# A four-layer graph kernel on one core: the input projected ahead of the first pass, and the second pass's first pieces loaded slot by slot

## The reference, cut to what matters

```python
# layer 0
h = jnp.maximum(_layernorm(x), 0.0)
A = a * adj + (1 - a) * I;  inv = 1 / A.sum(axis=1)
x = x + relu((inv[:, None] * A @ h) @ W0.T + b0)
# layer 1
h = jnp.maximum(_layernorm(x), 0.0)
XW = mobius_matvec(W1, h)                  # rows of h @ W1, rescaled by their norms
x = x + expmap0(relu(logmap0(mean(adj @ (gamma * XW), adj @ (gamma - 1)))))
# layer 2
h = jnp.maximum(_layernorm(x), 0.0) @ W2.T + b2
x = x + max over the rows h[topk_idx],  topk_idx = top_k(adj, 32)
# layer 3: as layer 1, with adj + I and a normalisation by degrees, then @ W3 + b3
```

## Time and profile before

| | us |
|---|---|
| three runs, median | 4701.98 |
| lowest, highest | 4695.71, 4706.68 |
| the profiled execution's own time | 4705.08 |
| its span, first to last instruction | 4703.3 |
| TensorE busy | 3573.1 (76% of the span) |
| VectorE, ScalarE, GpSimd busy | 2523.1, 1609.0, 2261.2 |

### The profile page before, as it was taken

How to read it: one execution, slowest core, us unless ns; L and a number is a source line. 1 busy time by engine, 2 the same in 40 slices (tenths; PEclk the granted TensorE clock), 3 DMA queues, 4 the chain that set the end, 5 groups by cost and what they waited for, 6 DMA issues and landing times.

```text
span 4703.3 us, 75636 instructions
## 1 busy us (share of the span) xinstructions
PE 3573.1 (76%) x29444; PEld 3486.2 (74%) x29444; DVE 2523.1 (54%) x5491; ACT 1609.0 (34%) x3554; POOL 2261.2 (48%) x2023
## 2 busy tenths in 40 slices
PE   6999999999999998576685771266666555666695
PEld 6999999999999998576685771266665555565695
DVE  5678878878878210343423416354444335344567
ACT  5777878778786221111201102111100000000114
POOL 4898989899897002334324324533333433323200
PEclk9999999999999999787886885587777777777897
DMA  7999999999999887465574662255555554555673
GB/s 240 332 393 363 385 359 381 356 386 379 367 389 360 283 292 261 154 230 179 199 248 154 221 219 82 84 201 180 178 188 168 171 179 156 176 188 181 207 252 106
DMA packets 401321, 1155.19 MB, mean 246 GB/s; under 512 B 36717, under 2 KB 56110, under 8 KB 401006
## 3 DMA queue, kind: packets, MB, share of 16 engines
q1 hardware_dynamic: 360096, 1082.21, 64.0%
q0 software_dynamic: 31360, 64.29, 5.1%
q10 hardware_dynamic: 9550, 4.69, 0.3%
HBM read 874.19 MB, written 276.86 MB: 245 GB/s over the span
## 4 chain that ended last, share of the span: by engine, by line
PE 61%; issue 20%; DVE 15%; ACT 2%; DMA 1%; POOL 1%; DVEq 1%; another core or an unknown queue 0%; ACTq 0%; SPq 0%
PE psU L628 17%; PE psT L714 16%; PE psT L746 11%; PE psT L614 7%; PE psU L714 5%; PE psU L746 4%; DVE agg L1653 3%; DVE HT L1649 2%; DVE D L1442 1%; DVE GR L1812 1%; DVE W L1653 1%; POOL D L495 1%; ACT ATS L858 1%; DMA adj_turned<-ATS 1%; DVE agg L1658 0%
## 5 line engine op out<-in xcount | busy, mean ns | idle before, releaser
L495 POOL TENSOR_TENSOR D<-D,iota 128x512 f32<-128x512 f32 x1024 | 1317.3, 1317 | 174.1 <-ACT D L865 153.7
L503 POOL DMA_INDIRECT D<-h_table,idx_own x624 | 596.3, 956 | 1665.5 <-DVEq L59 1229.6
L746 PE MATMUL psT<-ATS,PIECES 128*128 128x129 f32 x6144 | 875.6, 288 | 520.8 <-issue 392.6
L746 PEld LDWEIGHTS psT<-ATS,PIECES 128*128 128x128 f32 x6144 | 805.0, 204 | 550.3 <-issue 534.5
L628 PE MATMUL psU<-HB,ATS 128*128 128x129 f32 x8192 | 1013.0, 277 | 53.9 <-ACT ATS L858 51.9
L628 PEld LDWEIGHTS psU<-HB,ATS 128*128 128x128 f32 x8192 | 964.7, 193 | 64.0 <-ACT ATS L858 34.5
L714 PE MATMUL psT<-GR,PIECES 128*128 128x129 f32 x6144 | 840.8, 284 | 219.3 <-issue 213.0
L714 PEld LDWEIGHTS psT<-GR,PIECES 128*128 128x128 f32 x6144 | 779.9, 200 | 238.5 <-issue 238.4
L1442 DVE MAX8 D<-D 128x8 f32<-128x512 f32 x1024 | 643.9, 683 | 278.8 <-POOL D L495 269.2
L858 ACT ACTIVATE ATS<-psT 128x512 f32<-128x512 f32 x1024 | 556.1, 596 | 249.5 <-PE psT L614 190.1
L865 ACT ACTIVATE D<-PIECES 128x1024 f32<-128x1024 f32 x512 | 543.5, 1062 | 0.0
(11 more groups left out here) (404 smaller groups left out, 2866.1 us busy)
## 6 DMA issues: line engine op xcount, KB each, us to landing
PIECES<-adj_turned SPq DMA_DIRECT2D x512, 1024.0 KB
PIECES<-in_adj SPq DMA_DIRECT2D x256, 1024.0 KB
adj_turned<-ATS SPq DMA_DIRECT2D x512, 512.0 KB, 8.0
D<-h_table,idx_own POOLq DMA_INDIRECT x624
h_table<-HB ACTq DMA_DIRECT2D x8, 512.0 KB, 6.7
...
```

The costliest lines, as they stand in the source:

```text
L495: pool.tensor_tensor(key, key, iota[:, :], ALU.mult).then_inc(keyed, 1)
L503: pool.indirect_dma_start(slot, None, rows, bass.IndirectOffsetOnAxis(ap=index, axis=0)).then_inc(done, inc)
L746: last = nc.tensor.matmul(acc(h, r), block_of(slot, b, r), Hc[par][:, jj, :], start=(jj == 0 and opens(r)), stop=(jj == CT - 1 and closes(r)))
```

## The change

The five parts of x become units 0-2, 2-6, 6-10, 10-14, 14-16. All sixteen units are projected before the pass; the turned rows go to the two psT buffers in turn, the projected ones to psX and psY. VectorE, ScalarE and TensorE start the pass only when all units are taken. GpSimd waits for pass_ready before it writes its constants. The squares go to SQ (in D) and no longer to G. The interleaving of LayerNorm parts, projections and held-back masks in the first group is gone. SP waits for scanned (first two rows of the group's first piece scanned) where it waited for prefix_seen. At the end of the first pass SP issues each of the second pass's first four loads as soon as the slot's piece is stored, turned and masked. No line of the gathers (L502 to L581) is touched. The diff, with the one-line removals of unused names left out:

```diff
@@ -312,6 +310,7 @@
         pick_step = sem("pick_step")
         act_step = sem("act_step")
         piece_loaded = [sem(f"piece_loaded{i}") for i in range(SLOTS)]
+        pass_ready = sem("pass_ready")
         pair_transposed = sem("pair_transposed")
         pair_copied = sem("pair_copied")
         pair_used = sem("pair_used")
@@ -375,12 +374,8 @@
 
         block = ctx.enter_context(nc.Block())
         LOADS = 8 * 16
-        PARTS_IN = [(0, 2), (2, 4), (4, 8), (8, 12), (12, 16)]
+        PARTS_IN = [(0, 2), (2, 6), (6, 10), (10, 14), (14, 16)]
         ROWS_IN = [slice(first * TPG, end * TPG) for first, end in PARTS_IN]
-        AHEAD = 2
-
-        def part_of(u):
-            return [n for n, (first, end) in enumerate(PARTS_IN) if first <= u < end][0]
         HALF = [slice(0, NT // 2), slice(NT // 2, NT)]
         UNITS = NG
         STORED = 16 * (PAIRS // NAT)
@@ -433,21 +428,24 @@
                     sp.wait_ge(pair_transposed, 4 * (n - SLOTS + 1))
                     sp.wait_ge(masked, 2 * (n - SLOTS + 1))
                     if (n - SLOTS) % NPC == 0:
-                        sp.wait_ge(prefix_seen, (n - SLOTS) // NPC + 1)
+                        sp.wait_ge(scanned, 2 * (n - SLOTS) + 1)
                 sp.dma_start(pieces[n % SLOTS], adj_v[n // NPC, n % NPC, :, :, :]).then_inc(piece_loaded[n % SLOTS], 16)
-            for n in range(NPIECES - SLOTS, NPIECES):
-                store_pairs(n)
-
             def load_wide(q, s, k):
                 sp.wait_ge(piece_multiplied, q + 1)
                 sp.dma_start(slot_v[q % SLOTS], turned_v[s, k, :, :, :]).then_inc(piece_loaded[q % SLOTS], 16)
 
-            sp.wait_ge(pair_transposed, 2 * PAIRS)
-            sp.wait_ge(masked, 2 * NPIECES)
+            for i in range(NAT):
+                sp.wait_ge(pair_stored[i], STORED // NSG)
+            for k in range(SLOTS):
+                n = NPIECES - SLOTS + k
+                store_pairs(n)
+                sp.wait_ge(pair_transposed, 4 * (n + 1))
+                sp.wait_ge(masked, 2 * (n + 1))
+                load_wide(k, 0, k)
             for s in range(NSG):
                 for i in range(NAT):
                     sp.wait_ge(pair_stored[i], STORED * (s + 1) // NSG)
-                for k in range(NP):
+                for k in range(0 if s else SLOTS, NP):
                     load_wide(s * NP + k, s, k)
                 if s == 0:
                     general_rows()
@@ -481,6 +479,7 @@
             pool.memset(pfxn[PREFIX:HEAD, :], FAR_BELOW).then_inc(extra_constants, 1)
 
             pool.wait_ge(extra_constants, 4)
+            pool.wait_ge(pass_ready, 1)
             pool.memset(ones, 1.0).then_inc(pick_constants, 1)
             pool.memset(taken, -7.0).then_inc(pick_constants, 1)
             pool.iota(row_base, [[STRIDE, TPG]], base=-PREFIX, channel_multiplier=0,
@@ -588,19 +587,33 @@
             nc.tensor.transpose(psX[:, P:2 * P], wnat[:, 1, :], ident[:, :]).then_inc(weights_transposed, 1)
 
             def turn_h0(u):
-                pe.wait_ge(h0_ready, part_of(u) + 1)
-                if u:
-                    pe.wait_ge(h0_taken, u)
+                for c, (first, _) in enumerate(PARTS_IN):
+                    if u == first:
+                        pe.wait_ge(h0_ready, c + 1)
+                if u >= 2:
+                    pe.wait_ge(h0_copied, u - 1)
                 for r in range(TPG):
-                    last = nc.tensor.transpose(psX[:, r * P:(r + 1) * P], H[:, u * TPG + r, :], ident[:, :])
+                    last = nc.tensor.transpose(psT[u % 2][:, r * P:(r + 1) * P], H[:, u * TPG + r, :], ident[:, :])
                 last.then_inc(h0_turned, 1)
 
             def project_h0(u):
                 pe.wait_ge(h0_copied, u + 1)
+                if u >= 2:
+                    pe.wait_ge(h0_taken, u - 1)
                 for r in range(TPG):
-                    last = nc.tensor.matmul(psX[:, r * P:(r + 1) * P], HT[:, u % 2, r * P:(r + 1) * P],
+                    last = nc.tensor.matmul((psX, psY)[u % 2][:, r * P:(r + 1) * P], HT[:, u % 2, r * P:(r + 1) * P],
                                             W[0][:, :], start=True, stop=True)
                 last.then_inc(h0_out, 1)
+
+            def first_rows():
+                for first, end in PARTS_IN:
+                    turn_h0(first)
+                    for u in range(first, end):
+                        if u + 1 < end:
+                            turn_h0(u + 1)
+                        if u == 0:
+                            pe.wait_ge(weights_copied, 2)
+                        project_h0(u)
 
             def turn_pair(K):
                 n, h = K // 2, K % 2
@@ -617,8 +630,6 @@
 
             def add_pair(K):
                 g, k = K // NP, K % NP
-                if g == 0:
-                    pe.wait_ge(h0_taken, k // 2 + 1)
                 if g and k == 0:
                     pe.wait_ge(agg_copied, g)
                 for b in range(2):
@@ -650,15 +661,13 @@
                 last.then_inc(pj_out, 1)
 
             def adjacency_pass():
+                pe.wait_ge(h0_copied, NG)
                 turn_pair(0)
+                pe.wait_ge(h0_taken, NG)
                 for K in range(PAIRS):
                     if K + 1 < PAIRS:
                         turn_pair(K + 1)
                     add_pair(K)
-                    if K % 2 and AHEAD + K // 2 < NG:
-                        turn_h0(AHEAD + K // 2)
-                    if K % 2 == 0 and 0 < K // 2 and AHEAD + K // 2 - 1 < NG:
-                        project_h0(AHEAD + K // 2 - 1)
                     for b, (first, end) in enumerate(PREPS[:-1]):
                         turned_from = end * NP + 20 + 2 * (end - first)
                         for u in range(first, end):
@@ -808,10 +817,7 @@
 
             pe.sem_inc(piece_multiplied, SLOTS)
             pe.sem_inc(sums_added, 2)
-            pe.wait_ge(weights_copied, 2)
-            for u in range(AHEAD):
-                turn_h0(u)
-                project_h0(u)
+            first_rows()
             adjacency_pass()
             turned_pass()
             chunk_products()
@@ -834,16 +840,27 @@
                 act.wait_ge(h0_turned, u + 1)
                 if u >= 2:
                     act.wait_ge(h0_out, u - 1)
-                nc.scalar.activation(HT[:, u % 2, :], psX[:, :], ACT.Copy).then_inc(h0_copied, 1)
+                nc.scalar.activation(HT[:, u % 2, :], psT[u % 2][:, 0:GROUP], ACT.Copy).then_inc(h0_copied, 1)
 
             def take_h0(u):
                 act.wait_ge(h0_out, u + 1)
                 nc.scalar.activation(H[:, u * TPG:(u + 1) * TPG, :],
-                                     psX[:, :].rearrange("p (r f) -> p r f", f=P), ACT.Copy).then_inc(h0_taken, 1)
+                                     (psX, psY)[u % 2][:, :].rearrange("p (r f) -> p r f", f=P), ACT.Copy)\
+                    .then_inc(h0_taken, 1)
+
+            def first_rows(c, root=None):
+                first, end = PARTS_IN[c]
+                copy_h0(first)
+                for u in range(first, end):
+                    if u + 1 < end:
+                        copy_h0(u + 1)
+                    take_h0(u)
+                    if root is not None and u == first + 1:
+                        root_rows(root)
 
             def square_rows(c):
                 act.wait_ge(x_centred, c + 1)
-                nc.scalar.activation(SQ0[:, ROWS_IN[c], :], H[:, ROWS_IN[c], :], ACT.Square).then_inc(x_squared, 1)
+                nc.scalar.activation(SQ[:, ROWS_IN[c], :], H[:, ROWS_IN[c], :], ACT.Square).then_inc(x_squared, 1)
 
             def root_rows(c):
                 job(sm[:, 1, ROWS_IN[c]], sm[:, 0, ROWS_IN[c]], ACT.Sqrt)
@@ -921,23 +938,11 @@
                 job(sm[:, 5, ts], sm[:, 5, ts], ACT.Tanh)
 
             def adjacency_pass():
-                prep, masks_left = iter(()), iter(range(PAIRS))
-                LN_AT = {0: [(square_rows, 3)], 1: [(root_rows, 2)], 2: [(square_rows, 4)], 3: [(root_rows, 3)],
-                         5: [(root_rows, 4)]}
-                HELD, LATER = 6, 3
+                prep = iter(())
                 for K in range(PAIRS):
                     g, k = K // NP, K % NP
                     copy_pair(K)
-                    if K in LN_AT:
-                        for what, c in LN_AT[K]:
-                            what(c)
-                    masks = 1 if K < HELD or K >= HELD + 2 * LATER else 0 if K < HELD + LATER else 2
-                    for _ in range(masks):
-                        mask(next(masks_left))
-                    if K % 2 and AHEAD + K // 2 < NG:
-                        copy_h0(AHEAD + K // 2)
-                    if K % 2 == 0 and 0 < K // 2 and AHEAD + K // 2 - 1 < NG:
-                        take_h0(AHEAD + K // 2 - 1)
+                    mask(K)
                     if g and k == 0:
                         copy_sums(g - 1)
                         for first, end in PREPS:
@@ -1055,10 +1060,14 @@
```

(35 more changed lines are left out.)

2 lines of the change are left out of this document (removed).

## The result

The changed kernel takes 4672.55 us (median of five runs, 4671.63 to 4679.4), against 4704.58 us for the kernel before in as many runs beside it: ratio 0.9937, 95% interval 0.9922 to 0.9951, 32.0 us less. The forecast was 4677, from 4664 to 4694. The profiled execution took 4672.55 us, its span 4670.8 us.

A forecast was written before the change was run, and what follows sets the result against it. TensorE's work was taken as the largest part, 61% of the span, mostly first-pass products. 19 + 1.9 + 6.0 - 1.5 = 25.4 us less gave 4679.7 for the profiled execution, 4677 for the median; range 4664 to 4694.

The forecast's parts named there:

- Part 1: Prologue and first group: projecting all units ahead of the pass with double buffers ends group 0 at 144.9, 19 us gained.
- The walk: Prologue: step-by-step times of centring, spreading, clipping (clip) and roots per LayerNorm part, first add_pair at 60.5 us.
- the ramp of the ring: First group: allowance for a ramp in the ring of stores, gain taken as 19 instead of 19.6 us.
- Rival D: Prologue near VectorE's own bound, the pass starting at 53 to 56 us, whole kernel 4670; chance 0.10.
- Rival A: Prologue stays slow by low clock or ScalarE's order, first add_pair at 70 to 80, whole 4686 to 4696; chance 0.17.
- Part 2: First-pass group boundaries: SP's load wait comes 1.3 us later, 1.5 us lost; 1.9 us back at the first boundary.
- The ring: Store buffers in the first pass: SP waits up to 4.1 us cost nothing, then 0.67 us per us over about 4.3.
- the four late boundaries: First-pass boundaries 6, 9, 12 and 15: longer SP waits make TensorE wait, 3.1 us in all, taken as 1.5 lost.
- The 1.9 us of the first boundary: First pass: SP's 7.1 us wait, from held-back masks, becomes 2.5 + 1.3 and gives 1.9 us back.
- Rival C: First pass: scanning has no reserve, a lag stays and each boundary loses 3.2 us, whole 4725; chance 0.05.
- Part 3: Second pass start: loads slot by slot start TensorE 4.4 us sooner, 1.6 us from the clock, 6.0 us together.
- Gathers: Gather code: the change's short name speaks of gathers without pauses, but the diff holds no line of it; 0 us.

The follow-up runs named there:

- the run with one buffer: Changed kernel with each projection unit turned only when the one before is taken; 4689.3 against 4682.37 us of the kernel before, ratio 1.0015.
- the kernel without part 3: Changed kernel with the old end of SP's first-pass queue, second-pass loads after all stores and masks; 4653.93 against 4680.85 us of the kernel before, ratio 0.9937.
- part 3 alone: Kernel before with only the second pass's first four loads issued slot by slot; 4671.87 against 4680.85 us, ratio 0.9982.

## Why the prediction was right, point by point

**Part 1 (19 us; 19.8 came).** The walk held at nearly every step: clip 1 at 33.7 (32.0), clip 2 at 41.9 (41.4), clip 3 at 49.2 (48.8), first `add_pair` at 60.36 (60.5), group 0's sums at 144.8 (144.9). TensorE began part 1 at the lower level after 4.21 us of idling and turned to the upper one within it, by 37.5 us, as written. At clip 1 I was 1.7 us early: x's second part came at 9.57 us where I had 8.7, and one short step of centre 1 took 1.92 us where I had added some 0.5 for GpSimd's memsets. The lag was down to 0.5 by clip 2, before which VectorE already waited for ScalarE's root (0.46 us). Of the extra 0.8 us, 0.6 is the ramp of the ring that I had allowed for and that did not come. Rival D (pass at 53 to 56) needed a VectorE without waits, and it still waited for ScalarE's roots, 3.31 us for the last one. Rival A fell by the double buffers, as the run with one buffer shows.

**Part 2 (1.5 lost, 1.9 back).** The waits of SP were right to 0.1 us at 13 of 15 boundaries (the 12th was 5.4 us where I had 6.6, the 15th 5.1 where I had 5.4). The ring had a little more slack than I read: waits of 5.1 to 5.4 us cost TensorE between nothing and 0.4 us, where I had 0.6 to 0.8. The step that failed is the last one of this part. I reasoned that in three of the four late boundaries a late TensorE "waits there less" and still booked a loss. The runs show a gain of about 1 us in each preparation group, 3 to 6 in all, by steps of VectorE that run faster in a pause of GpSimd. It is a wrong sign of a small term. The earlier trace rows held the hint, the same clipping at 3.35 us beside GpSimd and at 2.29 without; I used it for the prologue only. The 1.9 us of the first boundary came back: SP waited 3.8 instead of 7.1 us there, and group 1 fell from 87.9 to 85.6 us. So the 15 groups should be some 6 us shorter; they are in the kernels with 1333.1 to 1336.8 us, but not in the first profile of the changed kernel, 1340.8. It has the gains of groups 1, 3, 6, 9 and 12 and lost 4.4 and 1.7 us in groups 14 and 15, where ScalarE waited 4.0 us for VectorE. Its second profile lost 2.3 in group 14; the kernel without part 3, the same code up to there, lost nothing. It varies from run to run, and its cause is open. So the 15 groups came out 0.6 us from the forecast only because two errors cancelled. Rival C, a lag of scanning that is never made up, did not occur: the plain boundaries waited 3.8 us from the first on.

**Part 3 (6.0 us; 5.8 came).** The start followed the copied sums at once, 4.4 us sooner; 1.4 us came from the clock. The kernel with this part alone gave the same two numbers.

**Later stretches (0; 7.1 came).** I wrote that I would be wrong if the time from the start of the second pass to the end changed by more than 5 us. It changed by 8.5: 1.4 is the clock that was in the sum, 6.6 lie in the stretch of the gathers, 0.5 in the tail. Between the second profiles of both kernels (spans 4679.6 and 4645.6 us, on two chips) the last two were 2.1 and 2.6. The same code took 2910.1 to 2917.7 us in the stretch of the gathers in eleven later profiles, some of the kernel before and some of changed ones, and these two ends are from one chip; so most or all of the 6.6 can be chance, and no edit of the change is shown to cause it. The tail is another matter: it is 129.2 to 130.9 us in the three profiles with the old VectorE program, and 128.3 to 128.8 in all eleven with the new one. In the three, VectorE stands idle for 0.50 us in line L1943 (L1946 in part 3 alone), in the eleven it does not, and TensorE then waits 1.97 instead of 1.61 us. In two of the three TensorE's records behind that wait are at the lower level, which makes some 1.6 us more. So some 0.4 us of the tail or more go with the change, though no line of it aims there; what makes VectorE idle is not shown. VectorE's idle time, and the same 12 records of TensorE in the kernel before and in the changed one, second profiles:

```profile
4579.56 2.60 DVE L1943 TENSOR_TENSOR HB<-GR,sm 128x1024 f32<-128x1024 f32 x2 [0.50 <-DVE HB L1943]
...
4587.44 2.51 PE L746 MATMUL psT<-ATS,PIECES 128*128 128x129 f32 x12
```

```profile
4555.06 1.50 PE L755 MATMUL psT<-ATS,PIECES 128*128 128x129 f32 x12
```

**Gathers**: costed at 0; no line of them was changed, and nothing shows an effect of their own.

So between the two profiles 32.5 us went where the sum had 25.4. The 7.1 us are 0.8 more from the prologue, 0.6 less from the 15 groups, 0.2 less from part 3, and 7.1 of later stretches that were not in the sum. Without these 7.1 the result would have been 4679.7, still within the range, and so it does not rest on them that the forecast held. Between the second profiles, 34.0 us apart, the stretches gave 18.7, 4.6, 4.4, 1.6, 2.1 and 2.6: parts 1 and 3 are there again, and the surplus lies elsewhere.
